# Order of the query-key projection, the turned strips and the turned rows inside each attention step

## The reference

```
q = _l2norm(proj(Wq)); k = _l2norm(proj(Wk)); v = proj(Wv)     # 16 heads of 16
attn = softmax(q k^T + bias)        # bias: 0 > rel or rel >= 128 masked, ALiBi slope per head
x = layernorm(x + (attn v) Wo^T)
h = gelu(x bw1^T + b1); x = layernorm(x + h bw2^T + b2)        # bw = mean|w| * sign(w), 1024 hidden
```

## Time and profile before

| | us |
|---|---|
| median of 3 runs | 403.35 (402.19 to 403.46) |
| profiled execution | 402.48 |
| its span, first to last instruction | 400.7 |
| PE, DVE, ACT, POOL busy | 370.3, 311.8, 312.5, 280.1 |
| steps 8 to 23 (16 steps), first scores at | 81.93 to 209.12 |

### The profile page before, as it was taken

One profiled execution on the slowest core, in us unless ns is written; L12 is line 12 of the kernel. 1 busy time (PEld: TensorE's weight loads), 2 busy tenths in 40 slices (PEclk: granted clock), 3 DMA queues, 4 the chain that ended last, 5 costly groups with the idle time before them and its releaser, 6 DMA issues. The chain is left out here.

```text
span 400.7 us, 11989 instructions
## 1 busy us (share of the span) xinstructions
PE 370.3 (92%) x3893; PEld 232.4 (58%) x3893; DVE 311.8 (78%) x854; ACT 312.5 (78%) x532; POOL 280.1 (70%) x424
## 2 busy tenths in 40 slices
PE   7588999999999999999999899889899999999991
PEld 5234655665566556655665556555566666666671
DVE  4964777687777877877778978646789988998985
ACT  3678787878887888788878778679888888888754
POOL 2387888888888888888888879969156635645321
PEclk9789999999999999999999999999999999999996
DMA  6687457643554355436533555431032126303112
GB/s 229 131 238 125 107 106 141 142 89 79 111 117 87 79 118 117 79 81 122 111 79 80 104 101 121 81 61 40 2 55 53 55 53 106 92 12 105 53 54 105
DMA packets 98542, 38.28 MB, mean 96 GB/s; under 512 B 84688, under 2 KB 97360, under 8 KB 98256
## 3 DMA queue, kind: packets, MB, share of 16 engines
q1 hardware_dynamic: 98512, 37.89, 42.9%
HBM read 12.72 MB, written 4.19 MB: 42 GB/s over the span
## 5 line engine op out<-in xcount | busy, mean ns | idle before, releaser
L1149 POOL TENSOR_SCALAR_AFFINE_SELECT prob<-prob 128x512 f32<-128x512 f32 x256 | 157.1, 645 | 34.8 <-ACT prob L601 34.8
L601 ACT ACTIVATE prob<-ps 128x1024 f32<-128x1024 f32 x128 | 127.3, 1027 | 3.1 <-PE ps L338 3.1
L365 PE MATMUL ps<-wqkv,xt 128*128 128x512 f32 x128 | 67.5, 615 | 2.3 <-DVE qkn L863 1.9
L511 PE MATMUL ps<-sgn,prob 128*128 128x256 f16 x512 | 61.5, 273 | 1.1 <-DVE prob L970 0.9
L485 PE MATMUL ps<-yT,sgn 128*128 128x512 f16 x256 | 61.1, 379 | 0.6 <-issue 0.6
L665 ACT ACTIVATE ps<-ps,bias,alpha 128x512 f32<-128x512 f32 x64 | 47.8, 750 | 15.6 <-PE ps L485 12.4
L511 PEld LDWEIGHTS ps<-sgn,prob 128*128 128x128 f16 x512 | 50.0, 98 | 14.4 <-DVE prob L970 2.6
L1206 POOL TENSOR_TENSOR resid<-z,resid 128x256 f32 (+1 forms) x31 | 22.6, 728 | 49.5 <-DVE z L980 49.5
L354 PE MATMUL ps<-prob,vdiag 128*17 128x128 f32 x1024 | 51.3, 274 | 2.5 <-POOL prob L1149 2.4
L338 PEld LDWEIGHTS ps<-qkT 64*128 64x128 f16 x512 | 17.7, 95 | 61.2 <-issue 34.6
L338 PE MATMUL ps<-qkT 64*128 64x256 f16 x512 | 45.8, 276 | 6.3 <-DMA qkT<-parts 5.2
(11 more groups left out here) (106 smaller groups left out, 578.2 us busy)
## 6 DMA issues: line engine op xcount, KB each, us to landing
xt<-in_xT SPq DMA_DIRECT2D x32, 128.0 KB, 2.9
resid<-in_x SPq DMA_DIRECT2D x32, 128.0 KB, 2.2
out_dram<-resid SPq DMA_DIRECT2D x7, 512.0 KB, 2.9
w_t<-in_w2T SPq DMA_DIRECT2D x1, 1024.0 KB, 8.4
w_t<-in_w1T SPq DMA_DIRECT2D x1, 1024.0 KB, 5.3
w_nat<-in_w SPq DMA_DIRECT2D x4, 256.0 KB, 4.8
wqkv<-in_wqkvT SPq DMA_DIRECT2D x3, 256.0 KB, 3.8
qkT<-parts SPq DMA_TRANSPOSE x32, 4.3
```

The source lines that it names most:

```text
L365: mm = nc.tensor.matmul(ps[:, QK[1 - par], :], xt[:, slot, k, :], wqkv[:, k, 0:2 * D], start=(k == 0), stop=(k == DC - 1))
L511: mm = nc.tensor.matmul(ps[:, banks[b], 0:D], hid[:, par, a, k, P * b:P * b + P], sgn2[:, k, :], start=(m == 0), stop=(m == 2 * HC - 1))
L601: nc.scalar.activation(prob[:, par, CH * c:CH * c + CH, :], ps[:, SC + 2 * (c % 2):SC + 2 * (c % 2) + 2, :], ACT.Exp, scale=QK_SCALE ** -2 ...
L1149: sel = nc.gpsimd.affine_select(out=at, in_=at, compare_op=ALU.is_ge, fill=0.0, base=-near, pattern=[[0, CH], [1 if near else -1, P]], cha ...
```

## The change

On PE, in each step that still projects (steps 0 to 28), half 0 of `project_qk` stands ahead of `turn_strips`, except in steps 26 and 27, where it keeps its place behind `turn_bound` and `means_taken`; and half 1 stands ahead of `turn_rows`. On ACT, `take_rows` stands behind `exps(2)` in place of ahead of it, in all steps that have it (2 to 31). No instruction is added or removed.

```diff
--- before.py
+++ after.py
@@ -400,21 +400,24 @@
                                           start=(k == 0), stop=(k == DC - 1))
                 mm.then_inc(wo_done, 1)
 
-            def step(i, par, slot, pv=True, prev2=True, prev3=True, next1=True, next3=True, between=None, before_pv=None):
+            def step(i, par, slot, pv=True, prev2=True, prev3=True, next1=True, next3=True, between=None, before_pv=None,
+                     qk_first=True):
 
                 scores(i, 0, par, slot)
                 scores(i, 1, par, slot)
+                if next3 and qk_first:
+                    project_qk(i, par, (slot + 3) % XS, 0)
                 if prev2:
                     turn_strips(i)
                 if between:
                     between()
-                if next3:
+                if next3 and not qk_first:
                     project_qk(i, par, (slot + 3) % XS, 0)
                 scores(i, 2, par, slot)
+                if next3:
+                    project_qk(i, par, (slot + 3) % XS, 1)
                 if prev2:
                     turn_rows(i)
-                if next3:
-                    project_qk(i, par, (slot + 3) % XS, 1)
                 scores(i, 3, par, slot)
                 if next1:
                     project_v(i, (slot + 1) % XS, prev3)
@@ -521,8 +524,8 @@
 
             step(NB - 8, 0, 0)
             step(NB - 7, 1, 1)
-            step(NB - 6, 0, 2, between=turn_bound, before_pv=spread_bound)
-            step(NB - 5, 1, 3, between=means_taken)
+            step(NB - 6, 0, 2, between=turn_bound, before_pv=spread_bound, qk_first=False)
+            step(NB - 5, 1, 3, between=means_taken, qk_first=False)
             step(NB - 4, 0, 0)
             step(NB - 3, 1, 1, next3=False, between=first_hidden)
             step(NB - 2, 0, 2, next3=False, between=lambda: hidden(0, 1, 0))
@@ -606,9 +609,9 @@
                 exps(1)
                 if early2:
                     high_halves(i, par)
+                exps(2)
                 if prev2:
                     take_rows(i)
-                exps(2)
                 if next3:
                     squares(i, par)
                 exps(3)
```

## The result

| | before | changed |
|---|---|---|
| median, 20 runs of each | 402.99 us (401.26 to 404.24) | 404.78 us (403.48 to 407.46) |
| profiled execution (span) | 402.48 (400.7) | 404.11 (402.4) |

The ratio is 1.0048, 95% interval 1.0033 to 1.0063: slower by 1.9 us (the two medians are 1.8 apart), where 402.8 us was forecast, too little to tell from no change. A repetition of the changed kernel (experiment 8) gave 404.32 and 1.0033 [1.0013, 1.0053].

What follows compares the result with a forecast made beforehand. PE was taken as the bound, 7.95 us a step, about 0.24 of it waiting for ACT's strips copy. Terms -2.4, +0.8, +0.7, +0.1, -0.05, -0.2, +0.5 sum to about -0.6: 402.8 us from 403.35, range 400.0 to 405.2.

Steps and rivals of the forecast that it cites:

- Steps 8 to 23: Loop: PE's wait for the strips' copy goes, net -0.15 us a step, 16 steps, -2.4 us.
- the cost of the new neighbours: PE's two swaps in each step: weight loads exposed behind scores cost 0.05 us each, together 0.10 per step.
- rival C: Loop: the strips' wait stays as the rows' wait for `otok`, 0.1 to 0.2 a step; chance 0.20 together with Rival B.
- Covered: Rows turned later on PE: strips to rows takes 1.82 us against 1.77, so no wait for `otok`.
- ACT's 0.88 covers it: Loop: ACT's idle 0.88 us a step absorbs the 0 to 0.3 us that DVE passes on.
- DVE's wait of 0.68 takes up most: Loop: strips reach DVE 0.7 us later; its idle wait for the squares absorbs most, leaving 0 to 0.3 us.
- Steps 24 to 27: End of loop: +0.7 us for steps 24 and 25, +0.1 for 26 and 27, which pay the second swap.
- the term of +0.7: Steps 24 and 25: strips 0.67 us later pass through DVE in full to PE's L456; bounds -0.3 and +0.95.
- Steps 2 to 7: Early steps: step 2 +0.10, later halves wait for landing x, mainly steps 5 and 6; sum +0.8 us.
- Steps 28 to 31: Last steps: 28 and 29 together -0.05 us, step 30 -0.2, step 31 +0.5.
- step 31: Rows' copy about 0.8 us later delays outputs and weighted sums on PE: +0.5 us, bounds 0 and +0.8.
- Rival B: Loop: later strips make DVE and ACT the bound, taking all 0.15 a step, 405.2 us; chance 0.20 with rival C.

Runs made afterwards that it cites:

- experiment 14: Changed kernel with DVE scaling v and resid ahead of `double`, where it idled for POOL: 403.09 us, ratio to before 1.0008.
- The probe: One more DVE instruction (0.64 us, result unread) in steps 4 to 23, in the changed kernel and in the one before: 413.59 and 410.71 us.
- 1: Changed kernel with half 0 behind the turned strips again in steps 24 and 25: 404.27 us, ratio to before 1.0041.
- 9: Changed kernel with before's order on PE in steps 2 to 7, steps 4 to 7 written out: 405.77 us, ratio to before 1.0071.
- 2: Kernel before with only ACT's copy of the rows moved behind `exps(2)`, PE's order untouched: 403.23 us, ratio to before 1.0008.
- 6: Changed kernel with DVE's two sums over w1 ahead of `double` in steps 24 and 25: 403.27 us, ratio to before 1.0015.
- 5: Changed kernel with each quarter of w1 loaded behind the next load of x on SP, steps 4 to 7: 405.02 us, ratio to before 1.0048.
- 12: Changed kernel with one more DVE instruction in steps 4 to 23, whose result nothing reads: 413.59 us, one run.
- 10: Changed kernel with half 0 ahead of the strips in step 26 too: 403.20 us, ratio to before 1.0010.
- 4: Kernel before with PE's new order in steps 24 and 25 only: 404.21 us, ratio to before 1.0032.
- 11: Changed kernel with the edits of 6, 9 and 10 and the rows ahead of the third exponential in step 31: 400.86 us, ratio to before 0.9957.
- the eight experiments named above: Experiments 1, 5, 6, 7, 9, 10, 11 and 12, which have the change in steps 27 to 31: that stage took 33.19 to 33.24 us.
- 7: Changed kernel with the edits of 5 and 6 and the rows ahead of the third exponential in step 31: 402.29 us, ratio to before 0.9993.
- 16: Changed kernel with the edits of experiment 14 and 10 and the rows ahead of the third exponential in step 31: 402.25 us, ratio to before 0.9981.
- 17: As 16, with half 0 waiting for xt alone and half 1 for resid on its own semaphore: 401.43 us, ratio to before 0.9969.
- 18: As 17, with before's order on PE in steps 2 to 7, steps 4 to 7 written out: 400.77 us, ratio to before 0.9949.
- 15: Kernel before with steps 4 to 7 of PE's program written out ahead of its loop: 403.70 us, one run.

## Why the forecast was wrong, point by point

*Steps 8 to 23: right.* -2.47 for -2.4; starts 7.80 us apart on average, no idle time before the strips. Where the cost of the new neighbours lies was read wrongly. Behind scores the half shows 1.12 us of records as said, but from start to start it takes 0.96 as ever (99.23 to 100.19); the 1.05 of the prediction was a half that stood behind transposes and had waited for x. What grew are the turned strips (0.53 for 0.49 in the mean of 16 steps) and rows (0.31 for 0.28, taken from experiment 14, where no `otok` holds them up), now that scores stand behind them: 0.08 together for 0.10. The Trainium skill's rule on weight loads pulled ahead (TensorE: Matmul & The Clock Gate, section on the array as 16 times 32x32) would have made the swaps free; with these 0.08 us the trace again doesn't quite agree. The gain was a little larger than said, 0.27 for 0.24, and rival C's wait of the rows for `otok` did come, at 0.03 us a step (124.73 against 124.20 in 14): "Covered" was wrong by that much.

*"ACT's 0.88 covers it", "DVE's wait of 0.68 takes up most": wrong, and the root of the rest.* A mean wait of the earlier trace rows was taken for slack. The probe measured 0.26 us a step of slack before (one kind of step took in all of it, the other grew by 0.78) and 0.1 after.

*Steps 24 to 27: the step that failed.* The forecast had +0.7 and +0.1 with +0.95 as the upper end of the first, from strips that come 0.67 later to an otherwise unchanged DVE. Measured +1.3 (experiment 8; 1 and 9 agree), +2.8 in the execution profiled first. In the repetition -0.14 lies in step 24, +0.59 in step 25 and +0.83 in step 26, and 0.5 comes with ACT's move alone (2). Two mechanisms are in it. The first is shown: DVE comes into steps 24 and 25 with no slack left, so its sums over w1 go into the time; moving them (6) or shortening the ring (14) takes 1.4 and 1.9 us away, putting half 0 back (1) takes nothing. What failed in the prediction is the term of +0.7: strips 0.67 us later were all that DVE was to pass on, and what the runs show is a DVE without slack, at +1.3. The second was in no term of the forecast: the later strips leave PE idle for 1.00 us in step 26 beside the 0.85 for w1, and in some executions the clock falls to 0.50 behind that, 1.6 us more. It did in two profiles (the changed kernel's and 5, both 12.31 us for the step) and didn't in 1, 8, 9 and 12 with the same idle times (0.98 in 1). With the hole filled (10) or made small (6, 14) no profile shows it. The mean granted clock of each of the other executions is on record, though not where in it the clock fell. It is 0.983 or less in 15 of the 20 runs of the changed kernel, with a median of 405.31 us, and 0.986 or more in five, with 403.93; of the 132 runs of the kernel before that stand beside the experiments 26 are that low. By these medians, as an estimate, about 0.9 us of the 1.9 comes with a lowered clock, and about 1 us stays without. In the repetition only 3 of 12 runs were low. Not all of these falls need lie in step 26: in the profiles of 1, 2, 4, 11 and 14 the clock fell in step 2, which then took 9.20 to 9.34 us and not 7.67 or 7.76.

*Steps 2 to 7: the sum right, the parts not.* +0.1 for step 2 and +0.80 (+1.04 in the repetition) for +0.7. Step 4, given 0, paid 0.23 with 0.40 us of waiting for x. Step 5, given +0.30, gained 0.16 with no wait for x. Step 6 waited: x was issued at 63.0, landed 4.0 later, and the half ran at 67.10; but it waited before too, and the step paid 0.01 us, not the +0.65 (in the repetition, with an idle time of 1.66, it paid 1.14). Step 7, given -0.1, paid +0.88: its x was issued at 72.59, 1.4 later than before, and landed at 75.8, for a half that ran at 75.89 with 0.97 of idle time. The half asks for x at about the time at which it lands: in step 10, with no other load about, resid lands at 96.8 + 2.2 = 99.0 and half 0 runs at 99.23. Before, resid landed at 94.8 + 2.1 = 96.9 for a half that ran at 99.18, so it had 2.3 us to spare. Before's order mends the stage (9: 39.71), so it is the earlier half; not w1 (5) and not the ring (14, where PE is faster and waits more). Why these x land after 3 to 4 us and not 2.2 isn't settled; w1, code packets and the other loads all lie beside them.

*Steps 28 to 31.* The -0.26 for -0.25 of the first profile was luck: the repetition has +0.28, and the eight experiments named above +0.23 to +0.26. The gain of step 30 came (7.23 for 7.48), but step 29 took 9.82 for 9.09: PE waits 0.71 us there for the rows' `otok`, a wait that the forecast had as covered. In step 31 the mechanism was right and the size a little large: PE's rows, answering to the earlier trace rows,

```profile
273.14 1.13 PE L399 MATMUL ps<-wo,oT 128*128 128x256 f32 x4 [0.80 <-ACT oT L593]
...
276.38 0.40 PE L354 MATMUL ps<-prob,vdiag 128*17 128x128 f32 x8
```

put the last quarter 7.05 us behind the step's first scores, for 6.67: +0.38, and +0.34 in the stage, for +0.5. Experiments 7 and 11 take it back.

*The sum.* The stages from step 3 to PE's end give +1.25 us with the fall of the clock and +0.5 without it; the ratios say +1.9 and +1.3. Much of the rest lies ahead of step 3: over the profiled executions of all kernels this stretch took 41.8 to 44.6 us, and the profile of before has nearly the shortest. It took 43.5 to 44.6 in the five with the fall of the clock in step 2 and 41.8 to 43.9 in the others. So 0.5 to 1 us of the difference between sums of stages and ratios is start-up and chance of single executions, which I can't assign to the change.

*Rival B* had the right sign and engine, not the mechanism. It put the loss in the loop, all of whose gain was to go. The loop kept its gain; the ring took its price from extras that stand beside it. That the measured 404.8 lies near its 405.2 is luck.

## What to carry over

A wait in the profile isn't slack. Where engines wait for one another in a ring, each can show idle time and none have slack; follow the chain round and add it up, or put a known amount of work into it: what of it doesn't lengthen the period is the slack, and look at single steps, as a mean can hide a step with none. Before bringing one engine's loop down to the length of such a ring, look for what is added beside it at the loop's ends, and for loads that were in time by less than the gain; those are where the price is paid, and moving the extras into the ring's own idle places (6, 14) took the loss of steps 24 to 27 away. Alone this only made the kernel even with the one before (1.0015, 1.0008); faster it became with the other repairs beside it (11, 16, 17, 18).

## What the runs showed of the hardware that I hadn't expected

- Transfers land later beside code that comes in: beside a packet of 16 KB of instructions a DMA transpose landed after 6.0 us for 4.3 (experiments 9 and 11), a load of 128 KB after 3.4 or 3.6 for 2.2 (9, 15). Beside four other packets the transpose landed after 4.6 or 4.7.
- After idle times of 1.00 and 0.85 us on PE in step 26 the granted clock fell from 1.00 to 0.50 for 3 us in two profiles and stayed at 1.00 in others with the same two idle times.
- PE busy for 124.73 of 124.73 us didn't mean that PE was the bound: with a shorter ring on three other engines the same instructions took 124.20.
- Float32 transposes with 64-row scores behind them take longer from start to start than with 128-row work behind them: four 0.53 us for 0.49, two 0.31 for 0.28 (means of 16 steps; the 0.31 from experiment 14).
